# Rotary attention of a two-layer decoder: products of the group two back, one maximum ahead of the scores and one behind, outputs taken a group later

## What is computed

```python
q, kv = split(x @ Wq), split(x @ Wkv)            # (16, 1024, 8)
freqs = _rotary_emb(n, DH, x.dtype)[None]
q, kv = _apply_rotary(freqs, q), _apply_rotary(freqs, kv)
q = q * SCALE
att = jnp.einsum('bmd,bnd->bmn', q, kv)
attn = jax.nn.softmax(att, axis=-1)
out = jnp.einsum('bij,bjd->bid', attn, kv)
out = out.reshape(b, H, n, DH).transpose(0, 2, 1, 3).reshape(b, n, dim)
return out @ Wout + bout
```

## Time and profile before

| | us |
|---|---|
| median of 3 runs | 4507.89 |
| lowest and highest of them | 4469.67, 4522.97 |
| the profiled execution | 4509.64 |
| its span | 4507.8 |
| the stage's groups in it (2907.9 to 3193.9) | 286.0 |
| TensorE busy in the span | 4254.3 |

### The profile page before, as it was taken

The page is one execution under the profiler, slowest core; times in us unless marked ns, Lnnn a source line. Parts: engine busy times, 40 slices in busy tenths (PEclk is TensorE's granted clock), DMA queues, the critical chain, the costliest instruction groups (busy, mean ns, idle before and its releaser), DMA issues. The chain is left out here.

```text
span 4507.8 us, 67257 instructions
## 1 busy us (share of the span) xinstructions
PE 4254.3 (94%) x25298; PEld 2317.3 (51%) x25298; DVE 2195.7 (49%) x2736; ACT 1817.5 (40%) x2105; POOL 3135.0 (70%) x1348
## 2 busy tenths in 40 slices
PE   6999799999999999999999978898899999999969
PEld 3555455555555555555555536433355555555436
DVE  4554555555454554545555302556555545455112
ACT  2333234444444444444444433244334444444422
POOL 3555368989898898989889980000068989899950
PEclk9999899999999999999999988766689999999979
DMA  1000000000000000000000001000000000000001
GB/s 34 6 5 3 4 2 2 2 2 2 2 2 3 2 2 2 2 2 2 2 1 2 1 1 35 24 1 1 4 2 2 2 2 2 2 1 2 1 13 31
DMA packets 25430, 23.65 MB, mean 5 GB/s; under 512 B 6321, under 2 KB 19106, under 8 KB 25122
## 3 DMA queue, kind: packets, MB, share of 16 engines
q1 hardware_dynamic: 23666, 17.05, 1.3%
q10 hardware_dynamic: 1456, 2.46, 0.2%
HBM read 18.97 MB, written 0.52 MB: 4 GB/s over the span
## 5 line engine op out<-in xcount | busy, mean ns | idle before, releaser
L410 POOL TENSOR_TENSOR c_SUM<-c_SUM,c_PR 128x1024 f32<-128x1024 f32 (+1 forms) x1176 | 2793.0, 2375 | 264.0 <-ACT c_PR L490 158.9
L568 DVE TENSOR_REDUCE c_MX<-c_XB 128x2 f32<-128x1024 f32 (+2 forms) x1156 | 1394.2, 1206 | 1223.9 <-PE c_XB L690 1223.0
L490 ACT ACTIVATE c_PR<-c_S 128x1024 f32<-128x1024 f32 (+1 forms) x1224 | 1194.8, 1023 | 1695.3 <-PE c_S L735 1584.9
L753 PE MATMUL c_O<-c_PR,c_V 128*64 128x512 f32 (+1 forms) x4896 | 1196.6, 607 | 2.8 <-ACT c_PR L490 2.8
L753 PEld LDWEIGHTS c_O<-c_PR,c_V 128*64 128x64 f32 (+1 forms) x4896 | 293.9, 136 | 568.4 <-issue 394.1
L735 PE MATMUL c_S<-c_SH,c_ONE 64*128 64x512 f32 x2448 | 482.4, 389 | 0.0
L877 POOL TENSOR_TENSOR ln_RSTD<-ln_VE,ln_POWER 128x8 f32<-128x8 f32 x7 | 11.5, 1642 | 544.5 <-DVE ln_VE L864 544.5
L690 PE MATMUL c_XB<-c_KHM,c_QH 64*128 64x512 f32 x1632 | 368.8, 447 | 11.9 <-DVE c_MX L568 8.2
L735 PE MATMUL c_S<-c_QH,c_KHM 64*128 64x512 f32 x1728 | 348.2, 399 | 8.4 <-ACT c_PR L490 8.3
L735 PE MATMUL c_S<-c_QH,c_KLM 64*128 64x512 f32 x1728 | 341.4, 391 | 0.0
L735 PE MATMUL c_S<-c_QL,c_KHM 64*128 64x512 f32 x1728 | 341.1, 391 | 0.0
(11 more groups left out here) (255 smaller groups left out, 4513.6 us busy)
## 6 DMA issues: line engine op xcount, KB each, us to landing
f_W<-in_L_w SPq DMA_DIRECT2D x34, 256.0 KB, 2.7
CTX<-in_ctx ACTq DMA_DIRECT2D x12, 192.0 KB, 4.2
c_WQ<-in_L_xattn_Wq SPq DMA_DIRECT2D x12, 64.0 KB, 1.8
c_WO<-in_L_xattn_Wo SPq DMA_DIRECT2D x12, 64.0 KB, 1.9
c_WK<-in_L_xattn_Wk SPq DMA_DIRECT2D x12, 48.0 KB, 1.7
c_WV<-in_L_xattn_Wv SPq DMA_DIRECT2D x12, 48.0 KB, 1.7
X<-in_x SPq DMA_DIRECT2D x1, 512.0 KB, 6.1
a_WQ<-in_L_attn_Wq SPq DMA_DIRECT2D x8, 64.0 KB, 1.8
```

Source lines behind the costliest of these rows:

```text
L410: pool.tensor_tensor(out[0:kp], out[0:kp], tile[0:kp], ALU.add).then_inc(summed, 1)
L490: act.activation(PR[u % BUFS][0:kp, :, :].rearrange("p h q -> p (h q)"), S[u % 2][0:kp, :], ACT.Exp)\
L568: dve.tensor_reduce(MX[:, q:q + tiles, :, column], bank[:].rearrange("p (h k) -> p h k", h=2) [:, :, 0:tiles * m].rearrange("p h (q k) -> ...
L753: last = pe.matmul(O[ROWS[h], :], V[pair.par][0:kp, t, ROWS[h]], PR[u % BUFS][0:kp, h, :], start=t == 0, stop=t == TILES - 1)
```

## The change

Five edits, all in `small_attention`; the instructions are the same in number and shape.

1. TensorE's group is now: two maxima, products of the group **two** back, a third maximum, `tiles`, a packing job (`K`, `Q`), the fourth maximum, any other job (`M`, `T`, `B`, `Y`).
2. At the end, two products stand behind the loop instead of one.
3. In the table, `T`, `B`, `Y` move from groups 1, 3, 5 to groups 2, 4, 6, and `K0`, `K1`, `Q0`, `Q1` from 2, 4, 6, 6 to 1, 3, 5, 5.
4. VectorE does all four maxima of a group and then the job, where before the job stood between the second and the third.
5. ScalarE takes the output of a finished period ahead of the exponentials of group 1, where before it did so behind those of group 0.

```diff
             if p:
-                jobs[p, 1], jobs[p, 3], jobs[p, 5] = ("T", p - 1), ("B", p - 1), ("Y", p - 1)
+                jobs[p, 2], jobs[p, 4], jobs[p, 6] = ("T", p - 1), ("B", p - 1), ("Y", p - 1)
 ...
             if p % 2 == 0 and p + 2 < PERIODS:
-                jobs[p, 2], jobs[p, 4], jobs[p, 6] = ("K0", p // 2 + 1), ("K1", p // 2 + 1), ("Q0", p // 2 + 1)
+                jobs[p, 1], jobs[p, 3], jobs[p, 5] = ("K0", p // 2 + 1), ("K1", p // 2 + 1), ("Q0", p // 2 + 1)
             elif p % 2 and p + 1 < PERIODS:
-                jobs[p, 6] = ("Q1", p // 2 + 1)
+                jobs[p, 5] = ("Q1", p // 2 + 1)
 ...
                         g = p * GROUPS + t
-                        tiles(p, t)
                         units = units_of(p, t)
+                        job = jobs.get((p, t))
                         for k in units[:2]:
                             maximum(k)
-                        if (p, t) in jobs:
-                            side(jobs[p, t])
-                        if g:
-                            products(g - 1)
-                        for k in units[2:]:
+                        if g >= 2:
+                            products(g - 2)
+                        for k in units[2:3]:
                             maximum(k)
+                        tiles(p, t)
+                        if job is not None and job[0][0] in "KQ":
+                            side(job)
+                        for k in units[3:]:
+                            maximum(k)
+                        if job is not None and job[0][0] not in "KQ":
+                            side(job)
+                products(PERIODS * GROUPS - 2)
                 products(PERIODS * GROUPS - 1)
 ...
-                        units = units_of(p, t)
-                        for k in units[:2]:
+                        for k in units_of(p, t):
                             maximum(k)
                         if (p, t) in jobs:
                             side(jobs[p, t])
-                        for k in units[2:]:
-                            maximum(k)
 ...
+                        if t == 1 and p:
+                            take_output(p - 1)
                         for pair in range(2):
 ...
-                        if t == 0 and p:
-                            take_output(p - 1)
```

More of the change, by code:

```diff
@@ L954, in small_attention @@
             if p % 2 == 0 and p + 2 < PERIODS:
-                jobs[p, 2], jobs[p, 4], jobs[p, 6] = ("K0", p // 2 + 1), ("K1", p // 2 + 1), ("Q0", p // 2 + 1)
+                jobs[p, 1], jobs[p, 3], jobs[p, 5] = ("K0", p // 2 + 1), ("K1", p // 2 + 1), ("Q0", p // 2 + 1)
             elif p % 2 and p + 1 < PERIODS:
-                jobs[p, 6] = ("Q1", p // 2 + 1)
-        jobs[PERIODS, 1], jobs[PERIODS, 3], jobs[PERIODS, 5] = [(kind, PERIODS - 1) for kind in "TBY"]
+                jobs[p, 5] = ("Q1", p // 2 + 1)
+        jobs[PERIODS, 2], jobs[PERIODS, 4], jobs[PERIODS, 6] = [(kind, PERIODS - 1) for kind in "TBY"]
         number = {job: n for n, (_, job) in enumerate(sorted(jobs.items()))}
```

## The result

The changed kernel takes 4459.3 us (median of 14 runs, 4435.5 to 4471.7) against 4507.8 us before (14 runs, 4469.7 to 4523.0): a ratio of 0.9897, 95% interval 0.9876 to 0.9917. The profiled execution is one of the longer ones, 4468.4 us (span 4466.6).

A forecast was written before the change was run, and what follows sets the result against it. TensorE and VectorE waiting on each other was taken as the bound; +20.8 - 18.4 - 2 - 2 = -1.6 us on the profiled 4509.6, less 1.7 to the median, gave 4506.3 us, range 4472 to 4542.

The forecast's parts named there:

- The ring: TensorE and VectorE wait on each other through maxima and products: 4.75 us per jobless group at low clock, 3.31 at full.
- The clock's share: In the first seven periods, 21 of 56 groups at full clock and 35 at half, kept unchanged for the sum.
- rival B: Jobs fill TensorE's waits and the clock stays high in the stage: 34 low groups become high, -68 us, 4438; chance 0.1.
- Part 1: Order of the maxima: the fourth, behind the scores, comes late, +0.58 us per low-clock group, +0.05 at full; +20.8 us.
- Part 2: Jobs leave the path before the products and fill TensorE's wait: -18.4 us, and -2 us for the packing jobs.
- the lower bound: 0 us for the later fourth maximum, if it could start beside the scores; excluded by the program-order rule.
- rival C: The fourth maximum is not late, so its cost is 0 to half: -10 to -21 us, about 4490; chance 0.15.
- Part 3: Products two back and later output cost zero; the stage's first and last groups and period 7 gain -2 us.
- Rival A: Two maxima between `Y` and the products keep the clock low: +21 us, 4527, or +42, 4548, if all; chance 0.2.

The follow-up runs named there:

- h1: The changed kernel run again with nothing edited: 208.1 us for the groups at clock 0.97, kernel 4443.5 us, ratio 0.9896.
- f3: The kernel before, in its own order, with four unread transposes behind the scores of each of the first 56 groups: groups 228.5 us, kernel 4456.0 us, ratio 0.9883.
- e3: The kernel before with only the jobs moved behind the fourth maximum (TensorE) and fourth reduction (VectorE): groups 226.3 us, kernel 4446.8 us, ratio 0.9884.
- g1: The changed kernel with two 16-column reciprocals on VectorE between third and fourth reduction: groups 266.7 us at clock 0.69, kernel 4483.6 us, ratio 0.9898.
- g2: The changed kernel with the same two reciprocals plus four unread transposes in each group without a job: groups 219.8 us, kernel 4456.6 us, ratio 0.9895.
- e4: The changed kernel with products one group back instead of two: groups 276.7 us at clock 0.71, kernel 4490.1 us, ratio 0.9994.
- f5: The changed kernel with one 16-column reciprocal on VectorE between third and fourth reduction: groups 223.0 us at clock 0.89, kernel 4463.1 us, ratio 0.9879.

## Why the prediction was wrong

**The ring.** Right. In both kernels TensorE and VectorE follow one another through the maxima and the products, at 4.75 and 3.3 us.

**The clock's share: the step that failed first.** "I keep this share for the sum" put 21 of 56 groups at the full clock; the changed kernel has 40 in one profile and 52 in the other. At before's share of 35 and 21, its own mean lengths of 4.80 and 3.28 us would make 35 x 4.80 + 21 x 3.28 = 237 us of the first seven periods' 266, so the ring without the clock is worth 29 us (an estimate). The profile's 59 leave 30 for the clock, h1's 78 (286.0 - 208.1) leave 49. The forecast held the two apart, but shorter groups with the same work kept the clock up. f3 shows that more work at the same length does it (0.67 to 0.98, 57 us), and e3 that shorter job groups with the same work do (0.88); g1 and g2 point the same way in one profile each. What exactly brings the clock down stays open: e3's falls twice at 3.4 us a group. I had put this down as rival B with a chance of 0.1 and 4438 us. Its place and sign are right; its size is that of all low groups going high, and between 3 and 15 of them stayed low.

**Part 1: the size was wrong, 20.8 us for nothing.** The fourth maximum starts 0.61 us behind the third (2976.93 against 2976.32), beside the last score matmul, and the low-clock group without a job is 4.76, not 5.33. I had argued that the score of head 3 had to stand behind that of head 2. In the records three of the four scores start at once with the maximum (2976.33, x3), and the fourth 0.59 later (2976.92), together with u3. The late one is head 2's, on the maximum's own row quarter: a pair's second matmul is the one that signals ScalarE, so heads 1 and 3 carry the signal, and the late record has none. A matmul on a free row quarter started although an earlier one still waited for its own quarter. So the rule of the Trainium skill that I leaned on (TensorE: Matmul & The Clock Gate, "What overlaps and what doesn't": matmuls in program order at start and end) does not hold for these starts. I had also put its "only" too widely: the section says it of weight loads, and here the products start side by side as well, though all four use the same 128 rows (within 0.02 us, at 2979.22). Excluding the lower bound by that rule was the error: the bound was the answer, and rival C was right here.

**Part 2: right in kind, too small.** Job groups at the full clock are 3.30 with `Y`, where I had 3.70, and 3.36 behind `T`, where I had 3.65; VectorE's place behind the reductions costs next to nothing. At the low clock `T` and `B` groups are 4.79 instead of the 5.52 forecast. The packing groups of period 0 are 5.05 at the low clock, against 5.61 before and my 5.3; nothing is left of the 0.58 for part 1, but 0.3 of the job, which I had as hidden, is. With part 1 at zero and the share kept, my own sum would have been -22 against the 29 worked out above.

**Part 3: right in its zero, not in its -2.** Products two back and the late output take nothing away, but period 7 is 20.4 us against 20.1 before, so the gain hoped for there did not come. What I hadn't seen is that one group of distance was no longer free in the new order (e4, 50 us more in the profile).

**Rival A** did not come. Its reason, the two maxima between `Y` and the products, is in the timeline above (3022.34), and the clock stayed up all the same. **Rival B's** counter-argument, that TensorE never paused long before and still fell, shows only that pauses aren't the measure: the longest in the first seven periods before was 0.55 us in the trace, but for one of 1.46 at their end. In g1 the clock fell again and again with no pause over 0.55 us, and the longest of the changed kernel, where it stayed up, is as long (0.54).

## What to carry to other kernels

Where TensorE runs at half clock in part of a stage, work out the sum at both clock shares and not only at today's: an edit that takes a few tenths off each round with the same work in it can go along with a clock that stays up, and the clock's part here was as large as the edit's own or larger (30 to 49 us beside 29). A cheap test is to put useless matmuls into a wait of the ring and look at the clock (f3). In a ring like this one, small jobs belong into the wait of its engine and not ahead of the instruction that the ring goes through; e3 shows that this move alone was enough, and e4 that here products moved ahead of the scores needed a second group of distance to cost nothing.

## What was not expected of the hardware

- **Useless work made the kernel 1.2% faster** (f3, ratio 0.9883, 0.9828 to 0.9938): 224 more transposes, and the clock went from 0.67 to 0.98 over the stage.
- **A few tenths of a us went with the clock**: at a full-clock group of 3.30 (changed kernel) or 3.40 us (f5) it stayed up once risen, at 3.51 (g1, one profile) and 3.56 (e4) it fell again and again, with the same work on TensorE. It is no sharp limit: e3's fell twice at a mean of 3.4.
- **Matmuls on different row quarters passed one another at the start**, by the records: the score of head 3 starts 0.59 us ahead of that of head 2, which stands before it in the program and waits for its own quarter.
- **The same program rose to its full clock at different moments**: after 15 low groups in one profile and after 3 in another, 19 us apart in the stage. At the start of the first cross-attention it was low for 116 us in the one and for 31 and 10 us in the other.
